# Graph attention layer with sparse experts: edge scores by a masked product and one maximum out of PSUM, with wider target products

## The chip, the cores and the metric

The kernel runs on one core of one Trainium2 chip. The metric is the device time of one execution in microseconds (us). TensorE (PE in the profile; PEld is its weight load), VectorE (DVE), ScalarE (ACT), GpSimd (POOL) and the queue of SyncE (SP) run side by side and wait for each other on semaphores; 16 DMA engines move the data.

## The reference

A graph attention layer over 3125 nodes, 50000 edges and the self loops, and behind it a layer of 8 experts with the top 2 chosen. The change touches the attention scores:

```python
xp = (x @ W).reshape(N, H, C)                      # N = 3125, H = 4, C = 256
a_src = jnp.einsum('nhc,hc->nh', xp, att_src)
a_dst = jnp.einsum('nhc,hc->nh', xp, att_dst)
e = jax.nn.leaky_relu(a_src[src] + a_dst[dst], NEG_SLOPE)
m = jax.ops.segment_max(e, dst, num_segments=N)
ee = jnp.exp(e - m[dst])
z = jax.ops.segment_sum(ee, dst, num_segments=N)
alpha = ee / z[dst]
out = jax.ops.segment_sum(xp[src] * alpha[:, :, None], dst, num_segments=N)
```

Each edge needs four numbers of its source node, `a_src[src]`, and eight (`a_src` and `a_dst`) of its target.

## The kernel before

The program is seven blocks, one after the other, each with its own instruction list for every engine and a barrier behind it. The nodes are cut into 25 blocks of 125 rows (`ROWS`), the edges, sorted by target, into 416 visits of up to 128 edges (`VISITS`), each of which belongs to one block of targets.

**Projection** (block at L303). For each of the 25 node blocks i, TensorE multiplies the normalised rows by W in two 16-bit parts (`body(i)`, L1886), and VectorE takes the sums with `att_src` and `att_dst` out of PSUM (`node_sums`, L508), the low part (`lo_proj`, L493), and normalises the rows of a later block (`moments`, `normed`, `normed_low` L487). TensorE can turn the rows of block i+1 (L1904) only after `normed_low(i+1)`. Between these, VectorE does work for the edges: `edge_numbers` at i = 13 splits each source number into a node block `hi` and a row in it `lo`; `high_one_hots` (L598) at i = 17 to 24 writes `hi_oh`, for each edge a row of 25 zeros and ones; `build_first` (L609, L610) at i = 22 turns the first chunk of numbers into one-hot matrices. SP's queue holds the loads of x in order, the store of `lo` and of the target's row (L327, L328), and last the load of chunk 0 (L332).

**Scores** (block at L760). The visits are cut into 8 chunks of 52, each chunk into 13 groups of 4 (104 groups). A chunk's numbers are loaded by SP (L767): two copies that each write the same 13312 bytes (52 visits of 128 numbers, 16 bits) into all 128 partitions, one of `lo` and one of the target's row. There are two buffers, `stage` and `one_hots`, so the load of chunk i waits until TensorE has done chunk i-2 (`s_grp`). VectorE compares each copy with the partition number, in place (`build`, L776 and L777), and does so for chunk i+1 between groups 8 and 9 of chunk i. `build` waits for the load; the groups behind it on VectorE wait with it.

For each group TensorE forms, per visit, `s_ps` = one-hot of `lo` times all node terms `st16` (125 rows, 25 blocks x 4 heads = 100 columns, a high and a low part: L865, 8 products) and `d_ps` = one-hot of the target's row times the 16 columns of its block (L870, 4 products). VectorE multiplies `s_ps` by `hi_oh` into `pick` (L790) and adds up over the 25 blocks into `sT` (L800). ScalarE copies `d_ps` out (L827). There are two PSUM buffers of each: TensorE starts group n when L790 of group n-2 is done (`s_sel`). During chunks 0 and 1 TensorE also does parts of other products (`gram_part`).

**Behind it** come the maximum over each target's edges (L895), the weighted sums over the edges with indirect gathers (L1039), the node layer (L1180), the routing (L1477) and the experts (L1698). The change does not touch them.

## Time and profile before

| | |
|---|---|
| time, 3 executions | 2158.95, 2160.12 (median), 2163.76 us |
| profiled execution, first to last instruction (its span) | 2296.1 us |
| mean granted clock of TensorE in it | 0.919 |
| scores block in it, from the first load to the last L800 | 332 to 482.6 us |

The profile gives no time of its own for the profiled execution beyond its span; that span is 136 us above the median of the executions without the profiler, so sums are made in microseconds of the span and carried over as differences. The granted clock is in units of 2.4 GHz (0.5 is 1.2 GHz). In a line of the time line the first number is the start, the second the length; `x8` means 8 instructions merged into one line, and what stands in brackets is how long the engine was idle before it and what released it. A line of the table of stretches has, for each engine, the busy time and the count of instructions, then the granted clock, the mean busy share of the 16 DMA engines, and GB/s.

### The profile page before, as it was taken

What the parts mean: (1) busy time and instruction counts of PE and PEld (TensorE: products, weight loads), DVE (VectorE), ACT (ScalarE), POOL (GpSimd) and SP (SyncE); (2) the same over time, 40 slices, a digit from 0 to 9 for tenths busy, and PEclk for the clock granted to TensorE, in tenths of its full rate; (3) what the DMA queues carried; (4) which work ended last, traced back from release to release, by engine and by line L of the source; (5) the groups of instructions that cost most, each with busy time, mean ns of one, the idle gap of its engine ahead of it and who ended that gap; (6) DMA issues with size and microseconds to landing.
All of it is one profiled execution on the core that took longest, in us unless ns stands there. A gap on an engine that the chain in (4) does not pass through costs nothing. (4 is left out here: it accounts for less than half of the span.)

```text
span 2296.1 us, 53233 instructions
## 1 busy us (share of the span) xinstructions
PE 1959.2 (85%) x14846; PEld 1318.7 (57%) x14847; DVE 1470.6 (64%) x4341; ACT 1137.3 (50%) x2499; POOL 768.2 (33%) x943
## 2 busy tenths in 40 slices
PE   6999977667878888888888589983899999999997
PEld 4666545645766667777667455652454445555553
DVE  7988859987666666666666699867543443443333
ACT  4444421113666666676666566654543443443332
POOL 1020000022555555555555232321233333333332
PEclk9999976568999999999999889995899999999999
DMA  7444544403988888888888677746646556644542
GB/s 272 134 143 136 172 131 172 186 0 114 312 281 291 286 299 287 294 296 287 287 298 294 235 249 240 228 142 234 233 169 249 212 167 239 221 160 171 176 162 80
DMA packets 135664, 490.15 MB, mean 213 GB/s; under 512 B 16900, under 2 KB 17108, under 8 KB 133410
## 3 DMA queue, kind: packets, MB, share of 16 engines
q0 software_dynamic: 95568, 334.62, 43.5%
q1 hardware_dynamic: 31954, 125.15, 15.1%
q10 hardware_dynamic: 8064, 29.36, 3.7%
q8 instruction: 47, 0.77, 0.1%
q14 instruction: 31, 0.25, 0.0%
HBM read 419.17 MB, written 81.17 MB: 218 GB/s over the span
## 5 line engine op out<-in xcount | busy, mean ns | idle before, releaser
L1130 PE MATMUL main_ps<-rows,O 128*128 128x256 f16 x4992 | 619.2, 283 | 125.7 <-DVE acc L1066 66.3
L1113 ACT ACTIVATE O<-O,pk 128x128 f16<-128x128 f16 x1664 | 502.9, 387 | 246.1 <-DVE O L1083 203.5
L1130 PEld LDWEIGHTS main_ps<-rows,O 128*128 128x128 f16 x4992 | 480.9, 102 | 217.9 <-issue 72.8
L1052 POOL DMA_INDIRECT rows<-projected,idx x416 | 395.5, 951 | 325.2 <-PE small_ps L1135 202.9
L1087 DVE TENSOR_SCALAR O<-O,pk 128x128 f16<-128x128 f16 x1664 | 314.6, 273 | 15.0 <-issue 0.2
L1837 PE MATMUL x_h<-w_p,gram 128*128 x1344 | 307.1, 386 | 18.4 <-ACT gram L1787 7.6
L1852 PE MATMUL x_o<-w_p,gram 128*128 x1344 | 308.0, 379 | 1.4 <-ACT gram L1806 1.4
L1886 PE MATMUL pj_ps<-gram,xsT 128*125 128x512 f16 x1200 | 271.1, 385 | 8.8 <-ACT xsT L402 5.5
L1837 PEld LDWEIGHTS x_h<-w_p,gram 128*128 128x128 f16 x1344 | 131.6, 99 | 171.6 <-issue 31.5
L1886 PEld LDWEIGHTS pj_ps<-gram,xsT 128*125 128x125 f16 x1200 | 163.2, 139 | 104.7 <-ACT xsT L402 8.6
L1083 DVE TENSOR_SCALAR O<-iota,pk 128x128 f16<-128x128 f16 x416 | 109.4, 263 | 164.9 <-PE small_ps L1135 124.1
L1852 PEld LDWEIGHTS x_o<-w_p,gram 128*128 128x128 f16 x1344 | 129.2, 98 | 147.1 <-issue 1.6
L1795 ACT ACTIVATE h_g<-h_b 128x512 f32<-128x512 f32 x56 | 35.3, 630 | 301.7 <-DVE h_b L1767 301.7
L1732 POOL DMA_INDIRECT out_dram<-x_y,xi x56 | 57.5, 1027 | 349.8 <-DVE x_y L1760 349.8
L1895 PE MATMUL n_pj<-gram,PK 128*128 128x512 f16 (+3 forms) x900 | 156.2, 330 | 13.3 <-ACT PK L1343 13.3
L1757 DVE SCALAR_TENSOR_TENSOR x_o<-x_o,b_t 128x1024 f32<-128x1024 f32 x56 | 69.0, 1233 | 135.4 <-PE x_o L1852 132.2
L1787 ACT ACTIVATE gram<-x_tr 128x2048 f16<-128x2048 f16 x56 | 105.1, 1878 | 58.3 <-PE x_tr L1904 55.0
L1895 PEld LDWEIGHTS n_pj<-gram,PK 128*128 128x128 f16 x900 | 83.8, 99 | 82.5 <-ACT PK L1343 15.9
L1760 DVE SCALAR_TENSOR_TENSOR x_y<-x_o,gate_of_slot,x_y 128x1024 f32<-128x1024 f32 x56 | 71.9, 1284 | 69.4 <-DMA x_y<-out_dram,xi 62.1
L1217 POOL TENSOR_TENSOR PK<-n_xn,PK 125x1024 f16<-125x1024 f32 x25 | 53.3, 2130 | 165.6 <-DVE n_x L1267 151.7
L1767 DVE SCALAR_TENSOR_TENSOR h_b<-x_h,b_b 128x512 f32<-128x512 f32 x56 | 38.7, 690 | 107.1 <-PE x_h L1837 104.3
L378 POOL DMA_DIRECT2D projected_f<-xp_f x25 | 13.2, 527 | 247.7 <-ACT xp_f L396 247.7
(346 smaller groups left out, 2538.9 us busy)
## 6 DMA issues: line engine op xcount, KB each, us to landing
w_f<-in_L_ffn_W_dram SPq DMA_DIRECT2D x14, 2048.0 KB
b_t<-in_L_ffn_b_dram ACTq DMA_DIRECT2D x56, 512.0 KB
projected_f<-xp_f POOLq DMA_DIRECT2D x25, 500.0 KB, 3.7
projected<-xp POOLq DMA_DIRECT2D x25, 500.0 KB, 4.6
out_dram<-n_x SPq DMA_DIRECT2D x25, 500.0 KB
x_after_gnn_normed<-PK POOLq DMA_DIRECT2D x25, 500.0 KB, 9.1
xt<-in_x_dram SPq DMA_DIRECT2D x24, 512.0 KB, 3.3
n_own<-projected_f SPq DMA_DIRECT2D x24, 512.0 KB, 13.0
```

Source lines behind the costliest of these rows:

```text
L1052: pool.indirect_dma_start(out=rows[:, 4 * p + k, :, :].rearrange("k n d -> k (n d)"), out_offset=None, in_=xp_d[:, :], in_offset=bass.Indi ...
L1083: dve.tensor_scalar(O[:, k, 0, :], iota16[:, :], pk[:, p, k, 0:1], None, ALU.is_equal).then_inc(s_oh, 1)
L1087: ins = dve.tensor_scalar(O[:, k, 1 + h, :], O[:, k, 0, :], pk[:, p, k, 1 + h:2 + h], None, ALU.mult)
L1113: ins = act.activation(O[:, k, 1 + HEADS + h, :], O[:, k, 0, :], ACT.Copy, scale=pk[:, p, k, w:w + 1])
L1130: pe.matmul(main_ps[:, h * C:(h + 1) * C], O[:, k, 1 + HEADS * a + h, :], rows[:, 4 * p + k, b, h * C:(h + 1) * C], start=first and h % 2 ...
L1757: dve.scalar_tensor_tensor(o_ps[:, p, :], o_ps[:, p, :], 1.0 / WS, b2_t[:, p, :], ALU.mult, ALU.add).then_inc(s_ob, 1)
L1760: dve.scalar_tensor_tensor(y[:, p, :], o_ps[:, p, :], at1(gateT, i), y[:, p, :], ALU.mult, ALU.add).then_inc(s_eo, 1)
L1787: act.activation(xgT[:, p, :, :, :], tr_ps[:, :, :, :], ACT.Copy).then_inc(s_xT, 1)
L1837: ins = pe.matmul(h_ps[:, :], xgT[:, p, a, k, :], w, start=(k == 0 and a == b), stop=(k == KD - 1 and a == 1))
L1852: ins = pe.matmul(o_ps[:, p, n * 512:(n + 1) * 512], hT[:, p, a, f, :], w, start=(f == 0 and a == b), stop=(f == KF - 1 and a == 1))
L1886: ins = pe.matmul(out, lhs[:, a, k, :], rhs[:, b, k, :], start=(k == 0 and a == b), stop=(k == last - 1 and a == 1))
L1895: ins = pe.matmul(out[:, cols], lhs[:, a, k, :], rhs[:, b, k, cols], start=(k == 0 and a == b), stop=True, skip_group_check=True)
```

## The change

1. The source number is split by 116 in place of 125: `lo` = number within 116 (`LOW`), and the quotient (27 values, `HI`) into two digits, a high one of 3 values and a low one of 9 (`TENS`). The one-hot matrix of 128 rows now holds 116 rows for `lo`, 3 for the high digit and 9 for the low digit (`parts_of`). So the copy of `lo` writes 116 partitions, and two further copies write 3 and 9; the copy of the target's row stays at 128.
2. A matrix `terms` (128 rows, 27 x 4 = 108 columns, two parts) replaces `st16` in the product. Its first 116 rows are the node terms, spread anew by 50 small products at the end of the projection; its last 12 rows hold a large negative number wherever the column's digit is not the row's (`digit_mask`). The product thus gives the wanted terms in one of 27 places and very negative numbers in the others, and one maximum over the 27 out of PSUM (`TENSOR_REDUCE`) replaces the multiplication and the sum. `hi_oh`, `pick` and `high_one_hots` go; TensorE waits for that maximum (`s_got`) in place of L790.
3. The target products read 96 columns (`WIDE`) in place of 16, six node blocks of which the first is the wanted one; ScalarE still copies 16 of each.

```diff
-HI = -(-NODES // P)
+LOW, TENS = 116, 9
+HI = -(-NODES // LOW)
+DIGITS = HI // TENS + TENS
+MASK = -65504.0
...
+        src_row = sbuf(early_ctx, "src_row", [P, 1])
+        terms = sbuf(early_ctx, "src_terms", [P, 2, HI, HEADS], F16)
         dstV = sbuf(early_ctx, "dstV", [VP, ROW4])
-        st16 = sbuf(early_ctx, "node_terms_parts", [ROWS, BLOCKS, 4 * HEADS], F16)
+        AHEAD = WIDE // (4 * HEADS)
+        st16 = sbuf(early_ctx, "node_terms_parts", [ROWS, BLOCKS + AHEAD - 1, 4 * HEADS], F16)
...
+        def parts_of(lo, dl):
+
+            end = LOW + HI // TENS
+            return (lo[0:LOW], lo_d), (lo[LOW:end], third_d), (lo[end:P], unit_d), (dl, dloc_d)
...
+            spread_ps = t_ps[:, :, :].rearrange("p a b -> p (a b)")[:, 0:2 * HI * HEADS].rearrange("p (n a h) -> p n a h", n=2, h=HEADS)
...
+                            sp.dma_start(third_d.rearrange("(p r) n -> p (r n)", r=4), rowV[:, 2, :]).then_inc(s_vstore, 16)
+                            sp.dma_start(unit_d.rearrange("(p r) n -> p (r n)", r=4), rowV[:, 3, :]).then_inc(s_vstore, 16)
+                    sp.wait_ge(s_vstore, 64)
+                    sp.wait_ge(s_tr_ix, 2)
+                    for t, d in parts_of(stage_lo, stage_dl):
+                        sp.dma_start(t, d[0:CHUNK, :].partition_broadcast(t.shape[0])).then_inc(s_row[0], 16)
...
-                        link(dve.tensor_scalar(fV[:, 1, :], fV[:, 0, :], 1.0 / ROWS, -float(ROWS // 2) / ROWS, ALU.mult, ALU.add))
+                        link(dve.tensor_scalar(fV[:, 1, :], fV[:, 0, :], 1.0 / LOW, -0.5 * (LOW - 1) / LOW, ALU.mult, ALU.add))
...
-                        dve.scalar_tensor_tensor(fV[:, 2, :], fV[:, 1, :], -float(ROWS), fV[:, 0, :], ALU.mult, ALU.add)
+                        dve.scalar_tensor_tensor(rowV[:, 0, :], fV[:, 1, :], -float(LOW), fV[:, 0, :], ALU.mult, ALU.add)
+                        link(dve.tensor_scalar(fV[:, 2, :], fV[:, 1, :], 1.0 / TENS, -0.5 * (TENS - 1) / TENS, ALU.mult, ALU.add))
+                        link(dve.tensor_scalar(fV[:, 2, :], fV[:, 2, :], WHOLE, None, ALU.add))
+                        link(dve.tensor_scalar(fV[:, 2, :], fV[:, 2, :], -WHOLE, None, ALU.add))
+                        dve.tensor_copy(rowV[:, 2, :], fV[:, 2, :])
+                        dve.scalar_tensor_tensor(rowV[:, 3, :], fV[:, 2, :], -float(TENS), fV[:, 1, :], ALU.mult, ALU.add)
...
-                    def high_one_hots(n):
-
-                        if n == 0:
-                            dve.wait_ge(s_trc, 2)
-                        vs = slice(n * CHUNK, (n + 1) * CHUNK)
-                        dve.tensor_tensor(hi_oh[:, vs, :], iota16[:, 0:HI].unsqueeze(1).broadcast_to([P, CHUNK, HI]),
-                                          hiT[:, vs].unsqueeze(2).broadcast_to([P, CHUNK, HI]), ALU.is_equal).then_inc(s_hioh, 1)
+                    def digit_mask():
+
+
+                        top = HI // TENS
+                        dve.memset(shift16[:, 0:P], 0.0)
+                        dve.memset(shift16[:, 2 * P:], 0.0)
+                        dve.tensor_copy(shift16[:, P:2 * P], ident)
+                        link(dve.tensor_scalar(digit[:, 0:1], iota_col[:, :], LOW - 0.5, -float(LOW), ALU.is_gt, ALU.mult))
+                        link(dve.tensor_scalar(digit[:, 1:2], iota_col[:, :], LOW + top - 0.5, -float(top), ALU.is_gt, ALU.mult))
+                        link(dve.tensor_tensor(digit[:, 2:3], digit[:, 0:1], digit[:, 1:2], ALU.add))
+                        link(dve.tensor_tensor(src_row[:, :], iota_col[:, :], digit[:, 2:3], ALU.add))
...
+                        link(dve.tensor_scalar(digits_of[:, 0, :], digits_of[:, 2, :], src_row[:, :], digit[:, 3:4], ALU.not_equal, ALU.mult))
+                        for part in range(2):
+                            dve.tensor_copy(mask[:, part, :, :], digits_of[:, 0, :].unsqueeze(2).broadcast_to([P, HI, HEADS]))
...
-                        if i in (15, 17, 19):
+                        if i in (15, 17):
                             turned_numbers((i - 15) // 2)
+                        if i == 16:
+                            digit_mask()
                         if 14 <= i < 14 + KD:
                             low_wp(i - 14)
-                        if 17 <= i < 25:
-                            high_one_hots(i - 17)
...
+                    dve.wait_ge(s_spread, 1)
+                    dve.tensor_copy(terms[:, :, :, :], spread_ps)
...
+                    pe.wait_ge(s_trc, 2)
+                    pe.matmul(spread_ps, ident16[:, :], mask[:, :, :, :], start=True, stop=True, skip_group_check=True)
+                    for n, blocks in enumerate((range(LATE), range(LATE, BLOCKS))):
+                        pe.wait_ge(s_st16, 2 * n + 2)
+                        for b in blocks:
+                            for a in range(ROWS * b // LOW, (ROWS * (b + 1) - 1) // LOW + 1):
+                                w = P - (ROWS * b - LOW * a)
+                                ins = pe.matmul(spread_ps[0:LOW, :, a, :], shift16[0:ROWS, w:w + LOW],
+                                                st16[:, b, :].rearrange("r (n g h) -> r n g h", n=2, g=2)[:, :, 0, :],
+                                                start=False, stop=True, skip_group_check=True)
+                    ins.then_inc(s_spread, 1)
...
-            pick = sbuf(c, "pick", [P, 2, 4, HEADS, HI])
...
-                        for t, d in ((lo_b, lo_d), (dl_b, dloc_d)):
-                            sp.dma_start(t[p], d[CHUNK * i:CHUNK * (i + 1), :].partition_broadcast(P)).then_inc(s_row[p], 16)
+                        for t, d in parts_of(lo_b[p], dl_b[p]):
+                            sp.dma_start(t, d[CHUNK * i:CHUNK * (i + 1), :].partition_broadcast(t.shape[0])).then_inc(s_row[p], 16)
...
-                        dve.wait_ge(s_row[p], 32 * (j + 1))
-                        dve.tensor_scalar(lo_b[p], lo_b[p], iota_col[:, 0:1], None, ALU.is_equal)
+                        dve.wait_ge(s_row[p], 64 * (j + 1))
+                        dve.tensor_scalar(lo_b[p], lo_b[p], src_row[:, 0:1], None, ALU.is_equal)
...
-                            if not early(n, 2):
-                                dve.wait_ge(s_got, n - 1)
                             dve.wait_ge(s_grp, n + 1)
-                            dve.tensor_tensor(pick[:, b, :, :, :], s_ps[b][:, :, :].rearrange("k v (a h) -> k v h a", h=HEADS),
-                                              hi_oh[:, four(n), :].unsqueeze(2).broadcast_to([P, 4, HEADS, HI]), ALU.mult).then_inc(s_sel, 1)
-                            if not early(n, 1):
-                                total(n - 1, 1 - b)
-
-                    def four(n):
-                        return slice(4 * n, 4 * n + 4) if isinstance(n, int) else bass.ds(4 * n, 4)
-
-                    def total(n, b):
-                        dve.wait_ge(s_sel, n + 1)
-                        dve.tensor_reduce(sT[:, four(n), :], pick[:, b, :, :, :], AX.X, ALU.add).then_inc(s_got, 1)
-
-                    dve.wait_ge(s_hioh, 8)
+                            four = slice(4 * n, 4 * n + 4) if isinstance(n, int) else bass.ds(4 * n, 4)
+                            dve.tensor_reduce(sT[:, four, :], s_ps[b][:, :, :].rearrange("k v (a h) -> k v h a", h=HEADS), AX.X, ALU.max).then_inc(s_got, 1)
...
-                        act.activation(d, d_ps[p][:, 0:16 * HEADS].rearrange("k (v n h) -> k v n h", v=4, n=2), ACT.Copy).then_inc(s_got_d, 1)
+                        act.activation(d, d_ps[p][:, 0:4 * WIDE].rearrange("k (v n) -> k v n", v=4)[:, :, 0:4 * HEADS].rearrange("k v (n h) -> k v n h", n=2), ACT.Copy).then_inc(s_got_d, 1)
...
-                                pe.wait_ge(s_sel, n - 1)
+                                pe.wait_ge(s_got, n - 1)
                             for u in range(4):
                                 for part in range(2):
-                                    h0 = 2 * HEADS * part
-                                    pe.matmul(s_ps[(p + q) % 2][:, u, :].rearrange("k (a h) -> k a h", h=HEADS), lo_b[p][0:ROWS, 4 * q + u, :],
-                                              st16[:, :, h0:h0 + HEADS], start=(part == 0), stop=(part == 1))
+                                    pe.matmul(s_ps[(p + q) % 2][:, u, :], lo_b[p][:, 4 * q + u, :],
+                                              terms[:, part, :, :].rearrange("r a h -> r (a h)"), start=(part == 0), stop=(part == 1))
                             if not early(n, 2):
                                 pe.wait_ge(s_got_d, n - 1)
                             for u in range(4):
-                                ins = pe.matmul(d_ps[(p + q) % 2][:, 4 * HEADS * u:4 * HEADS * (u + 1)], dl_b[p][0:ROWS, 4 * q + u, :],
-                                                st16[:, bass.ds(block_of[u], 1), :].squeeze(1), start=True, stop=True)
+                                ins = pe.matmul(d_ps[(p + q) % 2][:, WIDE * u:WIDE * (u + 1)], dl_b[p][0:ROWS, 4 * q + u, :],
+                                                st16[:, bass.ds(block_of[u], AHEAD), :].rearrange("r b n -> r (b n)"), start=True, stop=True)
```

What moves on SP's queue, at the end of the projection and the head of the scores block. Before:

```order
L332 DMA stage<-src_lo_by_visit 128x6656 [waits ix_tr,ix_vstore]
L332 DMA stage<-dst_local_by_visit 128x6656
L767 DMA one_hots<-src_lo_by_visit 128x6656
L767 DMA one_hots<-dst_local_by_visit 128x6656
L767 DMA stage<-src_lo_by_visit 128x6656 [waits ed_grp]
L767 DMA stage<-dst_local_by_visit 128x6656
```

And with the change, in the same place (`src_high_digit_by_visit` and `src_low_digit_by_visit` are the new arrays of digits):

```order
L349 DMA stage<-src_lo_by_visit 116x6656 [waits ix_tr,ix_vstore]
L349 DMA stage<-src_high_digit_by_visit 3x6656
L349 DMA stage<-src_low_digit_by_visit 9x6656
L349 DMA stage<-dst_local_by_visit 128x6656
L818 DMA one_hots<-src_lo_by_visit 116x6656
L818 DMA one_hots<-src_high_digit_by_visit 3x6656
L818 DMA one_hots<-src_low_digit_by_visit 9x6656
L818 DMA one_hots<-dst_local_by_visit 128x6656
L818 DMA stage<-src_lo_by_visit 116x6656 [waits ed_grp]
L818 DMA stage<-src_high_digit_by_visit 3x6656
```

Each load is four copies in place of two, the first of 116 partitions; the wait for `ed_grp` (`s_grp`) stands at the same copy.

What moves on VectorE, around the first `build` of the scores block. Before:

```order
L800 TENSOR_REDUCE sT<-pick 128x16 [waits ed_sel]
L776 TENSOR_SCALAR one_hots<-one_hots,iota_col 128x6656 [waits ed_row1]
L777 TENSOR_SCALAR one_hots<-one_hots,iota_col 128x6656
L790 TENSOR_TENSOR pick<-s_ps,PK 128x400 [waits ed_grp,ed_got]
L800 TENSOR_REDUCE sT<-pick 128x16 [waits ed_sel]
L790 TENSOR_TENSOR pick<-s_ps,PK 128x400 [waits ed_grp,ed_got]
```

With the change:

```order
L840 TENSOR_REDUCE sT<-s_ps 128x16 [waits ed_grp] x8
L827 TENSOR_SCALAR one_hots<-one_hots,src_row 128x6656 [waits ed_row1]
L828 TENSOR_SCALAR one_hots<-one_hots,iota_col 128x6656
L840 TENSOR_REDUCE sT<-s_ps 128x16 [waits ed_grp] x13
L827 TENSOR_SCALAR stage<-stage,src_row 128x6656 [waits ed_row0]
```

One reduction out of `s_ps` stands for each pair of L790 and L800; `build` keeps its place between groups 8 and 9 (the first group is a row of its own, ahead of these) and its wait for the load (`ed_row1`, `ed_row0`).

On TensorE a group of chunk 0 was, before:

```order
L857 TENSOR_LOAD visit_blocks
L865 MATMUL s_ps<-node_terms_parts,stage 128x100 [waits ed_sel]
L865 MATMUL s_ps<-node_terms_parts,stage 128x100 x7
L870 ISA [waits ed_got_d]
L870 MATMUL d_ps<-node_terms_parts,stage 128x16
```

and is now:

```order
L895 TENSOR_LOAD visit_blocks
L902 MATMUL s_ps<-src_terms,stage 128x108 [waits ed_got]
L902 MATMUL s_ps<-src_terms,stage 128x108 x7
L907 ISA [waits ed_got_d]
L907 MATMUL d_ps<-node_terms_parts,stage 128x96
```

The same rows in the same order, with 108 and 96 columns, and `ed_got` in the place of `ed_sel`.

## Rows read from the trace of the kernel before

**Rows 1.** The page: busy us (share of the span) of each engine.

```profile
PE 1959.2 (85%) x14846; PEld 1318.7 (57%) x14847; DVE 1470.6 (64%) x4341; ACT 1137.3 (50%) x2499; POOL 768.2 (33%) x943
```

**Rows 2.** Table of stretches: the scores block.

```profile
332.00:480.00 148.00, 106.83 (x1482) 91.69 (x1483) 136.53 (x229) 24.01 (x106) 0.00 (x0) 0.58 0.41 162
```

**Rows 3.** Instruction groups, 357-480 us: busy us, mean ns | idle.

```profile
L790 DVE TENSOR_TENSOR pick<-s_ps,PK 128x400 f32<-128x400 f32 x90 | 51.6, 574 | 4.2 <-PE d_ps L870 1.1
...
L800 DVE TENSOR_REDUCE sT<-pick 128x16 f32<-128x400 f32 x91 | 50.7, 558 | 0.0
```

**Rows 4.** Time line, 402 to 412 us: groups, a build, the next load's issue.

```profile
402.24 0.63 PEld L865 LDWEIGHTS s_ps<-node_terms_parts,one_hots 125*128 125x128 f16 x8 [0.23 <-DVE pick L790]
...
403.32 0.63 PEld L865 LDWEIGHTS s_ps<-node_terms_parts,one_hots 125*128 125x128 f16 x8 [0.23 <-DVE pick L790]
...
405.06 1.95 DVE L776 TENSOR_SCALAR stage<-stage,iota_col 128x6656 f16<-128x6656 f16 x1 [0.23 <-DMA stage<-dst_local_by_visit]
...
411.47 0.32 SPq L767 DMA_DIRECT2D one_hots<-src_lo_by_visit  x1
```

**Rows 5.** Time line, the next build.

```profile
422.99 1.94 DVE L776 TENSOR_SCALAR one_hots<-one_hots,iota_col 128x6656 f16<-128x6656 f16 x1
```

**Rows 6.** Table of stretches: while a chunk's two copies run.

```profile
413.00:421.00 8.00, 7.19 (x96) 6.49 (x93) 7.50 (x16) 1.79 (x8) 0.00 (x0) 0.50 0.96 399
...
419.00:421.00 2.00, 1.79 (x26) 1.61 (x25) 1.93 (x5) 0.45 (x2) 0.00 (x0) 0.50 1.00 426
```

**Rows 7.** Stretches in which one SP copy runs: 104, 125 and 125 partitions.

```profile
177.00:177.80 0.80, 0.80 (x5) 0.51 (x4) 0.80 (x7) 0.40 (x1) 0.00 (x0) 1.00 0.80 230
...
1304.90:1305.70 0.80, 0.00 (x0) 0.00 (x0) 0.70 (x4) 0.00 (x0) 0.00 (x0) 0.50 0.29 113
...
1525.50:1527.50 2.00, 2.00 (x45) 2.00 (x42) 1.90 (x8) 0.20 (x1) 1.31 (x2) 1.00 0.30 94
```

**Rows 8.** Time line of SP: issues of the two copies of 125 partitions.

```profile
1303.72 0.29 SPq L1183 DMA_DIRECT2D n_bias<-in_L_gnn_bias_dram  x1
...
1524.02 0.27 SPq L1202 DMA_DIRECT2D out_dram<-n_x  x1
```

**Rows 9.** Time line, scores block's head: load 1, build, load 2.

```profile
332.07 0.32 SPq L767 DMA_DIRECT2D one_hots<-src_lo_by_visit  x1
...
350.25 1.94 DVE L776 TENSOR_SCALAR one_hots<-one_hots,iota_col 128x6656 f16<-128x6656 f16 x1
...
356.76 0.32 SPq L767 DMA_DIRECT2D stage<-src_lo_by_visit  x1
```

**Rows 10.** Time line, projection: load of chunk 0, build, TensorE.

```profile
268.81 0.34 SPq L332 DMA_DIRECT2D stage<-src_lo_by_visit  x1
...
277.48 10.75 PE L1886 MATMUL pj_ps<-gram,xsT 128*125 128x512 f16 x48
...
283.44 1.95 DVE L609 TENSOR_SCALAR stage<-stage,iota_col 128x6656 f16<-128x6656 f16 x1 [1.82 <-DMA stage<-dst_local_by_visit]
...
292.34 1.86 PE L1904 MATMUL tr_ps<-ident,xs 125*128 125x125 f16 x16 [4.11 <-DVE xs L487]
...
293.99 12.38 PE L1886 MATMUL pj_ps<-gram,xsT 128*125 128x512 f16 x48
```

**Rows 11.** Waits of TensorE, 130 to 330 us: total, times, longest.

```profile
PE tr_ps L1904 <- DVE xs L487: 6.9, 6, 4.1
```

**Rows 12.** Time line: a VectorE step on 104x512; 24 products of 96 columns.

```profile
172.41 0.43 DVE L548 TENSOR_SCALAR stage<-stage 104x512 f32<-104x512 f32 x1
...
1541.55 1.18 PE L1886 MATMUL n_sc<-Msim,PK 128*128 128x96 f16 x24
```

**Rows 13.** Time line: last build and last sums of the scores block.

```profile
458.54 1.94 DVE L776 TENSOR_SCALAR one_hots<-one_hots,iota_col 128x6656 f16<-128x6656 f16 x1
...
481.60 1.04 DVE L800 TENSOR_REDUCE sT<-pick 128x16 f32<-128x400 f32 x2
```

**Rows 14.** DMA issues: KB each, median us from issue to landing.

```profile
projected_f<-xp_f POOLq DMA_DIRECT2D x25, 500.0 KB, 3.7
```

42 lines of the change are left out of this document (25 added, 17 removed).

## The prediction

> **What bounds the kernel now.** I read the page first, then the table of stretches for the scores block, its instruction groups, and last the time line around one `build`. Over the whole span TensorE is the busiest engine [rows 1], but the change sits in the scores block, and there it is VectorE: 136.5 of 148 us busy, TensorE 106.8, at a mean granted clock of 0.58 [rows 2]. Per group VectorE spends 0.57 us in L790 and 0.56 in L800 [rows 3], which overlap a little; the groups come every 1.08 us, and TensorE sits idle 0.23 us before each, released by L790 [rows 4]. That is the row that invites the change.
>
> The second thing to see is who else is at the edge. The `build` at 405.06 begins 0.23 us late, released by its DMA, not by a VectorE step [rows 4]. The load after it is issued at 411.47 [rows 4] and its `build` begins at 422.99 [rows 5]: 11.5 us. So a chunk's period of 17.9 us (405.06 to 422.99) is as much a loop of loads as of groups: load 11.5, `build` 3.8 (two steps of 1.95, slightly overlapped), 2.6 until TensorE has done groups 11 and 12 and frees the buffer. 11.5 + 3.8 + 2.6 = 17.9. Nothing that shortens groups 0 to 8 shortens this loop. What the copies do inside the 11.5 us: the DMA engines are busy 0.96 to 1.00 of the time, at 399 to 426 GB/s for all 16 [rows 6].
>
> **What the change does to the loads, the main term.** The copy of `lo` is cut from 128 partitions to 116, with copies of 3 and 9 beside it. The bytes are the same; the number of DMA engines is not. A copy of 104 partitions on SP's queue held 0.80 of the engines, which is 13 of 16 (0.81), and 104 = 13 x 8; two of 125 partitions, a broadcast load and a store [rows 8], held 0.29 and 0.30, which is 5 of 16 (0.31), and 125 = 5 x 25; 128 partitions hold all 16 [rows 6, 7]. From these three I take it that a copy on this queue goes to the largest number of engines up to 16 that divides its partitions. 116 = 4 x 29: four engines, 29 rows of 13312 bytes each. Behind them on the same queue stand the copy of 3, that of 9, and 8 rows per engine of the target's copy. The busiest engine carries 29 + 1 + 1 + 8 = 39 rows; before it carried 16.
>
> A row takes 13312 bytes / 26.6 GB/s (426 / 16) = 0.50 us. The nearest other row is the broadcast of 125, 113 GB/s on 0.29 x 16 = 4.6 engines, 24.4 GB/s each, 0.55 us a row [rows 7]. I take 0.50, because it is the same copy with the same row length. Then 23 more rows are 11.5 us, and a load takes 23.0 (39 x 0.50 and the same 3.5 of issue and landing). The trace does not show whether the small copies share their engines with the 29 rows; if not, 37 rows, 22.0 us. That and 0.55 are the ends: 10.5 to 12.7 us more per load.
>
> The Trainium skill, "DMA: Bandwidth & Descriptors", section "Why a DMA increments its semaphore by 16 and not by 1", says that on the hardware queues a copy takes the lowest-numbered engines. By that rule the small copies do share, the sum stays at 39 rows, and the end with 37 falls away; no row here shows it.
>
> **The terms, in us, against the profiled span.**
> - Load 1 (scores block). Issued at 332.07, needed at 350.25 [rows 9]. It now lands at 332.07 + 23.0 = 355.1: +4.8.
> - Loads 2 to 7: each is waited for from its issue to its `build`, as shown. 6 x 11.5 = +69.0 (63 to 76). VectorE, TensorE and ScalarE all stand in that wait, since TensorE can be only two groups ahead of VectorE.
> - VectorE's saving, 104 x about 0.5 us, falls into that wait: 13 groups at about 1.1 us are 14 of the new 29.4 us of a period. What hides it is the load; without it, it would be the first rival below.
> - TensorE's added columns: a group had 8 x 100 + 4 x 16 columns, now 8 x 108 + 4 x 96 = 1248. At 1.2 GHz, which the 0.50 of these stretches is [rows 6], that is 1.04 us; at 2.4 GHz 24 products of 96 columns took 1.18 us [rows 12], so 12 take 0.55 to 0.6. In chunks 1 to 6 it hides under the load too. The two groups between `build` and the next issue become 0.56 + 0.1 + 2 x 1.05 = 2.8 at the low clock, before 2.6; at the high one 1.8. I take no change (-5 to +1 in all).
> - Behind the last `build`. From 458.54 to the last L800 at 482.6 it was 24.1 us [rows 13], 17 groups of them. At 1.2 GHz TensorE needs 1.05 a group, nothing is gained; if the clock comes up, up to 17 x 0.48 = 8. After an idle load wait TensorE starts low, so I take a quarter: -2 (-8 to 0).
> - Load of chunk 0 (projection). Issued at 268.81, `build_first` began at 283.44 after 1.82 us of waiting for it, and TensorE then stood 4.11 us for `xs`; its next 48 products took 12.38 us where they had taken 10.75 [rows 10]. The wait is exposed already, so the 11.5 comes on top: VectorE has `node_sums`, `lo_proj` and `normed_low` queued behind it, and TensorE waits for the last. TensorE's idle 4.1 becomes about 16, and I add 2 for a longer stretch at half clock. +13.5 (11 to 17).
> - `high_one_hots` gone. TensorE waited 6.9 us for `xs`, of which 4.1 is the wait above [rows 11]; the other 2.8 were caused by these steps. -3 (-4 to 0).
> - More number work: five steps on 104x512, as the 0.43 us one [rows 12], at i = 13, 2 us, and 18 tiny ones at i = 16, each between nothing and that 0.43, say half, 4 us. What hides both is that VectorE is a step ahead of TensorE there; if that cover is gone, +6. I take +1.
> - The two further stores of digits follow the same wait on SP's queue; the loads of x behind them have an iteration in hand: 0. The 50 spreading products at the end of the projection run while VectorE does the last sums and POOL the last stores: 0 (up to +2).
>
> Sum: 4.8 + 69.0 + 0 - 2 + 13.5 - 3 + 1 = **+83 us**. The profiled span would go from 2296 to 2379. The timed executions are 136 us shorter than that span; a wait for a transfer should be as long in them, so I carry the difference over: 2160 + 83 = **2243 us** (+3.8%). A difference of 0.2% is about what a measurement of this kernel can tell from none.
>
> **Rivals.**
> 1. Faster: SP's copies are dealt out over all 16 engines whatever their partitions. POOL's store of 125 rows, 500 KB, lands in a median of 3.7 us [rows 14], over 135 GB/s, more than five engines at 24.4 carry, so that queue does deal this way. The Trainium skill, in the same section, tells of such an exception for the software queue only; the trace agrees in both rows. Then the busiest engine has 8 + 1 + 1 + 8 = 18 rows, load 12.5, and with the high clock a period of 12.5 + 3.8 + 1.8 = 18.1: six times +0.2, the end -8, the projection (+1 for its load, -3, +1) -1: -8, **2152 us**. It decides if SP's copy of 116 shows a DMA share near 1.0. Against it: the 0.29 and 0.30, on this very queue. Chance 0.07.
> 2. Dealt evenly, but the clock stays at 1.2 GHz: TensorE becomes the bound with 1.05 us a group, period 12.5 + 3.8 + 2.8 = 19.1, six times +1.2, nine groups of chunk 0 at +0.3, projection -1: +9, **2169 us**. For it: the clock was 0.50 while TensorE was busy nine tenths. Chance 0.04.
> 3. Worse than forecast: four engines move only as much each as in the store of 125 rows, 94 / 4.8 = 19.6 GB/s [rows 7], 0.68 us a row. Load 3.5 + 39 x 0.68 = 30.0: 11.8 for load 1, 6 x 18.5 = 111, 20.5 in the projection, less 4: +139, **2299 us**. Against it: that was a write to memory, the loads are reads. Chance 0.05.
>
> **How the numbers follow.** The forecast, slower by 83, has 0.84. Its own range: all low ends together give 3.8 + 63 - 5 - 8 + 10.5 - 4 = +60, all high ones 6 + 76 + 1 + 17 + 6 + 2 = +108. 2218 to 2272 holds nearly all of it, and leaves the three rivals out. Faster by over 0.2% is rival 1 but for its errors, 0.06; same, what is left of rivals 1 and 2 near zero, 0.02; slower 0.92.
>
> **What would show it.** While the copy of 116 runs, the DMA share is 0.25 and the rate near 105 GB/s, after a first stretch with all engines; the landing of the target's copy goes from 11 to about 22 us; `build` waits some 12 us on `dst_local`'s or `lo`'s DMA, seven times; its period is 29 us; `TENSOR_REDUCE` takes about 0.6 us and never waits long except for `build`; TensorE's wait for `xs` at the end of the projection is near 16 us. The forecast is wrong if the share of that copy is near 1, or if the period stays at 18 us.

## The result, and the profile after

| | before | after |
|---|---|---|
| time, median (us) | 2159.67 (2158.95 to 2163.76, 4 runs) | 2273.97 (2269.27 to 2286.09, 4 runs) |
| ratio, 95% interval | | 1.053 (1.0497 to 1.0563) |
| profiled span (us) | 2296.1; of a second profile 2151.0 | 2267.6 |
| block of edge scores (us) | 150.5 | 252.0 |

Slower by 114 us, where 83 were forecast; 2274 lies 2 us above the range's end of 2272. The profiled span of before, 2296, was 136 us longer than its timed runs. A second profile of the same kernel, 2151.0, shows where most of it lies: in the weighted sums, which the change does not touch and on which no term rests, 752 us for 624. The waits of SP, which span the blocks (us in total, times, longest), first profile of before:

```profile
SPq L1039 <- PEq L1039: 752.3, 1, 752.3
```

The second profile of before, and the kernel after (the same place in its code):

```profile
SPq L1039 <- PEq L1039: 623.6, 1, 623.6
```

```profile
SPq L1076 <- PEq L1076: 622.9, 1, 622.9
```

So blocks are compared here, not spans. The table of stretches of after: the scores block, then the parts of one load (us, busy time of PE, PEld, DVE, ACT, POOL, clock, DMA share, GB/s).

```profile
343.00:595.00 252.00, 106.44 (x1488) 87.39 (x1488) 92.40 (x130) 24.13 (x107) 0.00 (x0) 0.68 0.35 95
380.00:388.00 8.00, 7.72 (x107) 5.64 (x105) 4.31 (x8) 1.67 (x8) 0.00 (x0) 1.00 0.91 205
388.00:390.00 2.00, 1.35 (x21) 1.12 (x21) 1.12 (x2) 0.35 (x2) 0.00 (x0) 1.00 0.53 157
390.00:404.00 14.00, 1.18 (x15) 0.90 (x15) 0.00 (x0) 0.45 (x2) 0.00 (x0) 0.63 0.26 97
```

Against [rows 2] VectorE fell from 136.5 us busy in 148 to 92.4 in 252, and TensorE's busy time stayed at 106, with more columns at a higher granted clock (0.68 for 0.58): the edit did to the two engines what it was written to do. The time went to the load. Fourteen of its microseconds have a DMA share of 0.26, four engines of 16, and in them TensorE is busy 1.2 us and VectorE not at all; before, a load had a share of 0.96 over the 8 us of [rows 6]. The second thing to read here is the first line of the load. All engines are at work, 0.91, but move 205 GB/s and not 399 to 426: rows nearly twice as long. That is what the forecast did not have.

The builds of after in the time line, to be held against [rows 4] and [rows 5]:

```profile
405.20 1.95 DVE L827 TENSOR_SCALAR stage<-stage,src_row 128x6656 f16<-128x6656 f16 x1 [15.77 <-DMA stage<-dst_local_by_visit]
...
438.98 1.95 DVE L827 TENSOR_SCALAR one_hots<-one_hots,src_row 128x6656 f16<-128x6656 f16 x1 [17.20 <-DMA one_hots<-dst_local_by_visit]
```

and the first issues of three loads on SP:

```profile
343.38 0.25 SPq L818 DMA_DIRECT2D one_hots<-src_lo_by_visit  x1
...
378.30 0.25 SPq L818 DMA_DIRECT2D stage<-src_lo_by_visit  x1
...
411.88 0.24 SPq L818 DMA_DIRECT2D one_hots<-src_lo_by_visit  x1
```

From 378.30 to 405.20 is 26.9 us, from 411.88 to 438.98 is 27.1. A chunk takes 33.8 us (build to build) where it took 17.9. VectorE's waits for these loads:

```profile
DVE one_hots L827 <- DMA one_hots<-dst_local_by_visit: 54.7, 4, 17.2
DVE stage L827 <- DMA stage<-dst_local_by_visit: 50.7, 3, 17.7
```

Seven waits, 105.4 us. The eighth load is the one in the projection: VectorE waits 19.65 us for it, and TensorE, for the `xs` behind, 19.70 (before 1.82 and 4.11 [rows 10]).

```profile
295.53 1.95 DVE L648 TENSOR_SCALAR stage<-stage,src_row 128x6656 f16<-128x6656 f16 x1 [19.65 <-DMA stage<-dst_local_by_visit]
```

```profile
304.42 1.86 PE L1941 MATMUL tr_ps<-ident,xs 125*128 125x125 f16 x16 [19.70 <-DVE xs L505]
```

The operation that replaced the product and the sum of [rows 3]:

```profile
L840 DVE TENSOR_REDUCE sT<-s_ps 128x16 f32<-128x432 f32 x104 | 62.2, 606 | 53.5 <-PE d_ps L907 53.2
```

0.61 us a group in place of 1.13.

### The profile page after: what moved, and what is told of

The parts are those of the page before. It is cut to its first block and busy times, and to the rows that moved or that the text cites. A ratio compares the mean times of both kernels' runs of the same rounds, so it can differ in the third digit from the quotient of the medians.

```text
span 2267.6 us, 53157 instructions
## 1 busy us (share of the span) xinstructions
PE 1901.3 (84%) x14894; PEld 1293.5 (57%) x14895; DVE 1420.2 (63%) x4253; ACT 1134.6 (50%) x2499; POOL 774.2 (34%) x943
## 3 DMA queue, kind: packets, MB, share of 16 engines
q1 hardware_dynamic: 32188, 125.36, 16.5%
## 5 line engine op out<-in xcount | busy, mean ns | idle before, releaser
L1167 PE MATMUL main_ps<-rows,O 128*128 128x256 f16 x4992 | 573.2, 273 | 46.4 <-DVE acc L1103 28.7
L1167 PEld LDWEIGHTS main_ps<-rows,O 128*128 128x128 f16 x4992 | 464.1, 98 | 112.6 <-DVE acc L1103 33.8
L1120 DVE TENSOR_SCALAR O<-iota,pk 128x128 f16<-128x128 f16 x416 | 116.6, 280 | 55.7 <-PE small_ps L1172 26.4
L865 ACT ACTIVATE d_p<-d_ps 128x64 f32 (+1 forms) x104 | 23.4, 225 | 236.7 <-PE d_ps L907 236.7
L902 PE MATMUL s_ps<-src_terms,stage 128*128 128x108 f16 x416 | 36.3, 245 | 82.1 <-DVE sT L840 66.4
```

The source lines that it names most:

```text
L1120: dve.tensor_scalar(O[:, k, 0, :], iota16[:, :], pk[:, p, k, 0:1], None, ALU.is_equal).then_inc(s_oh, 1)
L1167: pe.matmul(main_ps[:, h * C:(h + 1) * C], O[:, k, 1 + HEADS * a + h, :], rows[:, 4 * p + k, b, h * C:(h + 1) * C], start=first and h % 2 ...
```

## The experiments

Eighteen runs. In the table "rate" is what the stretch shows in a load's first part, while the lo copy or both run; "load" is from SP's first issue to the build that needs it, the mean of the loads of chunks 2 to 7; "period" from build to build, the mean of five (of four in e6). All are read from the time lines and tables of stretches. The time is the median of 4 to 10 executions in before, after, e1, e4, e5, e8 and e9; the others ran once.

| run | copies, partitions | rate, GB/s (share) | load, us | period, us | time, us |
|---|---|---|---|---|---|
| before | 128, 128 | 399 to 426 (0.96 to 1.0) | 11.6 | 17.9 | 2159.7 |
| after | 116, 3, 9, 128 | 205 (0.91) | 27.1 | 33.8 | 2274.0 |
| e1 | 112, 2, 14, 128 | 240 (1.02) | 14.6 | 21.3 | 2178.2 |
| e2 | 116, 12, 128, code of before | 223 (0.99) | 28.3 | 34.7 | 2283.1 |
| e3 | 128 first, 116, 3, 9 | 389 (1.02), then 92 (0.24) | 25.2 | 32.1 | 2257.6 |
| e4 | 128, 128, then 3, 9 over it | 422 (1.02) | 13.0 | 19.7 | 2164.7 |
| e5 | as e4, build later | as e4 | hidden | 16.3 | 2142.8 |
| e6 | as after, build later | | 33.5 | 27.1 | 2222.3 |
| e7 | 112, 16, 128, code of before | 240 (0.99) | 13.9 | 20.2 | 2171.1 |
| e8 | as e5, 16 columns | as e5 | hidden | 16.5 | 2141.9 |
| e9 | as before, build later | | hidden | 17.7 | 2158.8 |
| e10 | 116, 3, 9 alone | 100 (0.26) | 19.5 | 26.3 | 2229.5 |
| e11 | 128 and 128 on two queues | 407 (0.97) | 11.7 | 18.0 | 2166.8 |
| e12 | as after, one source | 216 (0.95) | 26.9 | 33.6 | 2277.0 |
| e13 | 116, 128 | 229 (1.04) | 25.9 | 32.7 | 2263.9 |
| e14 | 112, 112, 16, 16 | 283 (0.98) | 16.9 | 23.3 | 2196.5 |
| e15 | 104, 104 | 173 (0.81) | 17.7 | 24.0 | 2198.7 |
| e16 | 112, 112 | 300 (1.03) | 13.0 | 19.4 | 2169.3 |
| e17 | 104, 128 | 213 (1.00), then 359 (0.85) | 14.3 | 20.6 | 2171.2 |

**e0_before**, the kernel before, once more with a profile.

> The kernel before, profiled anew. Its first trace spans 2296 us, 136 above its times, and its block of weighted sums shows 752 us against 623 in the trace of the changed kernel, though neither kernel differs there. If that was a disturbance of one execution, this trace spans about 2160 to 2165 us, the block takes about 620, and the scores block again 150. If the block really is slower before, it stays near 750.

2152.8 us. Its weighted sums take 623.6 us, as shown above. Its scores block begins at 329.74 us, that of the first profile at 332.07: where the block begins is known to some 2 us.

**e1_low112**: is it the number of partitions?

```diff
-LOW, TENS = 116, 9
+LOW, TENS = 112, 14
```

> The changed kernel with 112 rows of lo, 2 of the high digit and 14 of the low one in place of 116, 3 and 9: the same computation, one line. Theory (rows on the busiest DMA engine): 7 + 1 + 1 + 8 = 17 rows in place of 39, a load of 12 us in place of 26.9, a period of 18 to 19 us in place of 34, in all 2150 to 2170 us. Rival (the number of copies, or the wider products, make the kernel slower): near 2274 us.

2178.24 us, ratio to before 1.0089 (1.0061 to 1.0116). One number gives back 96 of the 114 us; everything else of the change is still in. It missed its expectation by 8 us all the same: a load takes 14.6 us, not 12, with all 16 engines busy:

```profile
424.00:432.00 8.00, 5.87 (x97) 4.78 (x95) 4.85 (x8) 1.79 (x8) 0.00 (x0) 0.99 1.02 240
```

**e2_old_split**: is it anything else of the change? The kernel before with its lo copy cut in two, in chunk 0 as well.

```diff
-for t, d in ((lo_b, lo_d), (dl_b, dloc_d)):
-    sp.dma_start(t[p], d[...].partition_broadcast(P))
+for t, d in ((lo_b[p][0:116], lo_d), (lo_b[p][116:P], lo_d), (dl_b[p], dloc_d)):
+    sp.dma_start(t, d[...].partition_broadcast(t.shape[0]))
```

> The kernel before with only its copy of lo cut in two, 116 and 12 partitions, of the same array; everything else as before. Theory: 29 + 1 + 8 = 38 rows on the busiest engine, a load of 26 us, 2260 to 2275 us. Rival (the new arithmetic or the small arrays matter): 2160 us.

2283.1 us. The kernel of before, its arithmetic untouched, becomes slower than after by the cut alone. Its build, against [rows 5]:

```profile
514.24 1.95 DVE L776 TENSOR_SCALAR one_hots<-one_hots,iota_col 128x6656 f16<-128x6656 f16 x1 [16.47 <-DMA one_hots<-dst_local_by_visit]
```

With e1 this settles where the 114 us come from. The size of a load, 27.1 for 23.0, was still open.

**e3_target_first**: do the target's rows slow down when they run beside the 116?

```diff
-return (lo[0:LOW], lo_d), (lo[LOW:end], third_d), (lo[end:P], unit_d), (dl, dloc_d)
+return (dl, dloc_d), (lo[0:LOW], lo_d), (lo[LOW:end], third_d), (lo[end:P], unit_d)
```

> The changed kernel with the target's copy (128 partitions) issued ahead of the three others. The busiest engine still has 39 rows. In the changed kernel all 16 engines were busy for the first 8 us of a load at only 213 GB/s, a row taking 0.86 us and not 0.50. Theory A (the two copies disturb each other while they run side by side): issued in this order they hardly overlap, rows take 0.50, a load 23 us, in all 2274 - 8 x 3.9 = 2243 us. Theory B (rows are slower whenever few engines carry most of the work): no change, 2270 to 2278 us.

2257.6 us, between the two. The target's rows now run at the old rate, and then comes the copy on four engines, with a slow seam between them:

```profile
474.00:478.00 4.00, 3.71 (x54) 3.40 (x51) 2.55 (x5) 0.89 (x4) 0.00 (x0) 0.73 1.02 389
478.00:480.00 2.00, 1.39 (x26) 1.13 (x24) 1.22 (x2) 0.45 (x2) 0.00 (x0) 1.00 0.18 47
480.00:496.00 16.00, 2.53 (x44) 1.99 (x40) 1.22 (x2) 0.89 (x4) 0.00 (x0) 0.70 0.24 92
```

So side by side the two copies do cost each other time. A load gets only 1.8 us shorter where theory A had 3.9; the seam at 47 GB/s and rows at 92 GB/s (97 in the kernel after) take back the rest.

**e4_overwrite**: the change with an even copy. All 128 partitions are loaded from `lo_d`; the digits go over rows 116 to 127 when that has landed.

```diff
-return (lo[0:LOW], lo_d), (lo[LOW:end], third_d), (lo[end:P], unit_d), (dl, dloc_d)
+return (lo, lo_d), (dl, dloc_d), (lo[LOW:end], third_d), (lo[end:P], unit_d)
...
-for t, d in parts_of(lo_b[p], dl_b[p]):
+for n, (t, d) in enumerate(parts_of(lo_b[p], dl_b[p])):
+    if n == 2:
+        sp.wait_ge(s_low[p], 16 * (i // 2 + 2))
```

> The changed kernel with rows 0 to 127 of the lo copy loaded as one copy of all 128 partitions (as before the change), and the two small copies (3 and 9 partitions) written over its rows 116 to 127 once it has landed; nothing else moved. Theory (the four engines that carry 116 partitions are the whole loss): a load takes 12.5 to 14 us from issue to build, the period of a chunk falls from 34.0 to 19.5 to 20.5 us, 2155 to 2172 us in all. Rival (four copies of a load, or small ones, cost by their number): a load stays over 18 us and the time over 2200.

2164.74 us, ratio 1.0015 (1.0005 to 1.0026): the rate is back, a load takes 13.0 us, and four copies a load cost little by their number.

```profile
436.00:442.00 6.00, 4.15 (x71) 3.44 (x71) 3.65 (x6) 1.34 (x6) 0.00 (x0) 1.00 1.02 422
```

What is left is the change without its loss, and it is no gain: the loop of load 13.0, build 3.8 and 2.9 until the buffer is free sets its period, whatever VectorE saves.

**e5_over_later**: the loop taken apart.

```diff
-if q == GR - 4 and not (isinstance(i, int) and i == 7):
+if q == GR - 2 and not (isinstance(i, int) and i == 7):
```

> The same with VectorE's build of the next chunk put two groups before the chunk's end instead of four, so that TensorE finishes the chunk, and SP issues the load after the next, without waiting for that build. Theory: the load is no longer in one chain with the build, VectorE's own work (one maximum of 0.61 us a group, 13 groups, and the build) or TensorE's 13 groups set the period, 14 to 17 us against 17.95 before the change; 2125 to 2145 us in all, under the kernel before. Rival (the chain load, build, products stays, since only two buffers are there): the period stays 19 to 20 us and the time within 5 us of the run without the later build.

2142.78 us, ratio **0.9915** (0.9898 to 0.9931), the first version that beats both. TensorE finishes a chunk, and SP issues the load after the next, without waiting for the build between them. No build waits for a load:

```profile
417.32 1.95 DVE L832 TENSOR_SCALAR one_hots<-one_hots,src_row 128x6656 f16<-128x6656 f16 x1
...
433.48 1.95 DVE L832 TENSOR_SCALAR stage<-stage,src_row 128x6656 f16<-128x6656 f16 x1
```

16.2 us here: 13 groups at 1.04 and 2.6 more in which TensorE waits for the end of the build.

**e6_later_build**: the same edit, alone, on the kernel after.

> The changed kernel, its copies unchanged, with the build two groups before the chunk's end instead of four. Theory: a load still takes 26.9 us, but loads follow each other without the 7 us of build and products between them: period 28 to 29 us, 2235 to 2245 us. Rival (the load slows when its predecessor is still under way, since the same four engines carry both): 33 to 34 us a chunk and 2270 us as before.

2222.3 us, 13 us better than the better expectation: period 27.1 instead of 33.8. The load's own time is now hidden in part behind the one before. Its stretches hold a hint on the open question. In its load from 371 on, all 16 engines move 206 to 235 GB/s, as in the kernel after; at 396 to 398, when two loads overlap, the rate is whole:

```profile
396.00:398.00 2.00, 0.00 (x0) 0.00 (x0) 0.00 (x0) 0.00 (x0) 0.00 (x0) 0.50 1.00 419
```

The build at 399.96 waits for the load before, whose last rows on the four engines are the target's. If the order of a queue's rows on an engine is the order of issue, then at that moment all 16 engines carry rows of copies of 128 partitions.

**e9_old_later**: is the place of the build a gain by itself? Same edit, kernel before.

> The kernel before the change with its build put two groups before the chunk's end instead of four. Theory (its VectorE, with a product and a sum for each group, sets the period of 17.95 us, and no build waits over 0.23 us for a load): nothing to gain, 2155 to 2163 us. Rival (the place of the build alone made the gain of the fastest version): 2135 to 2150.

2158.84 us, ratio 0.9995 (0.9982 to 1.0008): nothing. The two edits of e5 need each other: the later build takes the load out of the loop, and only the single maximum lets the period fall below 17.7.

**e8_over_later_narrow**: e5 with the target products back to 16 columns.

```diff
-st16[:, bass.ds(block_of[u], AHEAD), :].rearrange("r b n -> r (b n)")
+st16[:, bass.ds(block_of[u], 1), :].squeeze(1)
```

ScalarE's copy reads the narrower PSUM rows accordingly.

> The fastest version so far (lo copy of 128 partitions with the small ones written over it, later build) with the target products back to 16 columns; everything else is the same. Theory of the widening (the added columns keep TensorE's clock up, and cost little): the granted clock of the scores block falls below its 0.88, groups follow each other at over 1.04 us, and the time rises by 3 to 15 us, to 2146 to 2158. Rival (the columns are work and nothing else): a group gets 0.05 to 0.15 us shorter at the same clock, and the time falls to 2128 to 2138.

2141.93 us, ratio to before 0.9924 (0.9898 to 0.9949), against 0.9915 of e5: no difference. The scores stretch of e5, then of e8:

```profile
343.00:468.00 125.00, 89.96 (x1300) 75.65 (x1298) 85.87 (x118) 22.95 (x102) 0.00 (x0) 0.88 0.46 172
```

```profile
343.00:468.00 125.00, 92.45 (x1264) 80.48 (x1263) 85.63 (x117) 22.87 (x101) 0.54 (x1) 0.70 0.45 172
```

The widening does raise the granted clock, 0.88 for 0.70. The theory was right on that and wrong on what it is worth: with a sixth of the columns in the target products and the lower clock TensorE is busy 92.5 us instead of 90.0, and the period is 16.5 us for 16.3. The time lines say why the clock buys nothing. Two groups of e5, then of e8:

```profile
429.06 0.56 PE L907 MATMUL s_ps<-src_terms,one_hots 128*128 128x108 f16 x8 [0.32 <-issue]
...
430.09 0.56 PE L907 MATMUL s_ps<-src_terms,one_hots 128*128 128x108 f16 x8 [0.29 <-issue]
```

```profile
425.84 0.90 PE L907 MATMUL s_ps<-src_terms,one_hots 128*128 128x108 f16 x8
...
426.86 0.90 PE L907 MATMUL s_ps<-src_terms,one_hots 128*128 128x108 f16 x8
```

The groups start 1.03 and 1.02 us apart here, 1.04 in the mean of a chunk in either run. In e5 the products are done sooner, and TensorE then stands 0.3 us marked "issue", for nothing that the profile shows. What holds the groups at 1.04 us no run separates.

**e7_old_112_16**: is every cut slow? The kernel before, lo copy as 112 and 16.

> The kernel before the change with its lo copy of 128 partitions issued as two, of 112 and of 16 partitions; the same rows into the same places. Both spread over all 16 engines, so the even share stays. Theory (a row costs more when the engines are out of step with each other, as between copies of 7 and 8 rows an engine): a load takes 14 us instead of 12.5, of which the kernel before hides most: 2160 to 2175 us. Rival (rows cost 0.5 us whatever their neighbours do): 2155 to 2160 us, load 12.5 to 13 us.

2171.1 us, load 13.9, as its theory expected (the theory itself falls below, with e14). All 16 engines are busy, and the rows are slow until the target's are alone:

```profile
399.00:407.00 8.00, 7.11 (x92) 6.50 (x92) 7.72 (x16) 1.56 (x7) 0.00 (x0) 0.50 0.99 240
407.00:411.00 4.00, 3.12 (x43) 2.75 (x40) 2.88 (x6) 0.89 (x4) 0.00 (x0) 0.50 0.88 367
```

**e10_lo_only** and **e11_two_queues**: the uneven copy without a neighbour, and two even copies side by side, the target's issued by ScalarE.

```diff
-for t, d in parts_of(lo_b[p], dl_b[p]):
+for t, d in parts_of(lo_b[p], dl_b[p])[0:4 if i == 1 else 3]:
```

> The changed kernel without the target copies of chunks 2 to 7 (their target one-hots are left out of the computation, the old ones stay); the lo copy of 116 partitions and the two small ones as they are. Theory (rows on the four engines take 0.50 us when no other copy runs beside them): 29 rows and the 3.5 us around them make a load of 18 us, a period of 25 us, some 2220 us in all. Rival (rows of this uneven copy are slow by themselves at its start): a load of 21 us or more, and 2240 us.

> The kernel before the change with the target copy issued by ScalarE on its own queue at the same moment as SP issues the lo copy, so that the two run side by side on all 16 engines with even shares. Theory A (two copies that read different places of HBM at once slow each other's rows, whatever their shares): rows take 0.8 to 1.0 us, a load 16 to 19 us, the time 2180 to 2210 us. Theory B (it takes engines with different shares or out of step, two sources alone cost nothing): a load stays 12 to 13.5 us and the time 2155 to 2165.

e10: 2229.5 us, load 19.5, 100 GB/s on four engines, 0.53 us a row, and no slow start (81 to 115 GB/s in any 2 us of it). The expectation of 18 had forgotten its own small copies: (29 + 1 + 1) x 0.50 + 3.5 is 19.0. e11: 2166.8 us, 2 above the range of theory B, with a load of 11.7 us, as before, and rows of 0.51 us.

```profile
409.00:423.00 14.00, 6.05 (x96) 4.94 (x96) 4.12 (x7) 2.32 (x10) 0.00 (x0) 0.84 0.26 100
```

```profile
397.00:403.00 6.00, 5.32 (x70) 4.88 (x71) 5.79 (x12) 1.17 (x6) 0.00 (x0) 0.50 0.97 407
```

Neither the copy of 116 alone nor two copies of 128 side by side makes rows slow. Here it takes both.

**e12_same_source** (target copy reads `lo_d` too) and **e13_no_small** (no copies of 3 and 9 from chunk 2 on).

```diff
-(lo[end:P], unit_d), (dl, dloc_d)
+(lo[end:P], unit_d), (dl, lo_d)
```

> The changed kernel with the target copy reading the same table as the lo copy (its one-hots of the targets are then those of the sources' low digit, so the sums by target are left wrong); copies, sizes and destinations are unchanged. Theory (two sources read at once by engines of different shares conflict in HBM): rows of 0.5 us in the first part too, over 350 GB/s there, a load of 23 us, 2243 to 2252 us in all. Rival (the sources do not matter): about 213 GB/s in the first 8 us, a load of 26 to 27 us, 2265 to 2278 us.

> The changed kernel without the small copies of 3 and 9 partitions in the loads of chunks 2 to 7 (their digits stay those of chunks 0 and 1, so the scores of later chunks are left wrong). Theory (the small copies put the engines out of step and keep the rows slow): over 350 GB/s in the first part, a load of 22.5 to 23.5 us, 2243 to 2252 us. Rival (they do nothing beyond their own rows): a load of 26 to 27 us, 2262 to 2276 us.

e12: 2277.0 us and 216 GB/s, so the sources do nothing. e13: 2263.9 us, 229 GB/s, a load of 25.9: the small copies cost 1.2 us of a load, about the 1.0 of their two rows on a busiest engine.

```profile
450.00:458.00 8.00, 5.87 (x98) 4.90 (x96) 4.25 (x7) 1.79 (x8) 0.00 (x0) 1.00 0.95 216
```

```profile
447.00:453.00 6.00, 4.26 (x72) 3.49 (x70) 3.68 (x7) 1.35 (x6) 0.00 (x0) 1.00 1.04 229
```

**e14_in_step**: kernel before, lo 112, target 112, lo 16, target 16.

> The kernel before the change with each of its two copies of 128 partitions cut into 112 and 16, issued as lo 112, target 112, lo 16, target 16: 7, 7, 1 and 1 rows an engine, so that both large copies have the same shares. Theory of step (rows slow down when the copies under way have different shares or start positions): back to rows of 0.50 to 0.54 us, a load of 12.5 to 13.2 us, 2157 to 2166 us. Rival (7 partitions between the engines instead of 8 make the rows slow): rows of 0.65 us or more, a load of 14 to 16 us, 2170 to 2185 us.

2196.5 us, slower than its rival's range too. Copies with the same shares are slow as well, so it does not take engines out of step:

```profile
413.00:423.00 10.00, 8.85 (x114) 8.06 (x115) 9.66 (x19) 2.21 (x10) 0.00 (x0) 0.50 0.98 283
```

**e15_both104**, **e16_both112**, **e17_lo104**: kernel before, its copies of chunks 2 to 7 cut to 104 and 104, 112 and 112, 104 and 128 partitions, nothing in place of the rest.

```diff
-for t, d in ((lo_b, lo_d), (dl_b, dloc_d)):
-    sp.dma_start(t[p], d[...].partition_broadcast(P))
+for t, d, k in ((lo_b, lo_d, P if i == 1 else 104), (dl_b, dloc_d, P if i == 1 else 104)):
+    sp.dma_start(t[p][0:k], d[...].partition_broadcast(k))
```

> The kernel before the change with both copies of chunks 2 to 7 cut to partitions 0 to 103 (the rest keep what chunks 0 and 1 left, so those scores are left wrong): 13 engines if the share is 8 rows each, partitions 8 apart. Theory of spacing (rows are fast where the engines write partitions 8 apart): rows of 0.50 to 0.52 us, about 345 GB/s in the middle of a load, the load 12 to 12.8 us, 2153 to 2162 us in all. Rival (anything but 128 partitions is slow): rows of 0.65 us or more, under 280 GB/s, a load of 14 us or more.

> The same with partitions 0 to 111: 16 engines, 7 rows each, partitions 7 apart, and no small copies at all. Theory of spacing: rows of 0.65 to 0.75 us, 260 to 320 GB/s, the load 12.6 to 14 us for 14 rows an engine. Rival (the extra copies of 16 partitions slowed the rows of the run in step): rows of 0.50 us, about 420 GB/s, the load 10.5 to 11 us, shorter than with 104 partitions.

> The same with 104 partitions in the lo copy and all 128 in the target copy: 16 rows on 13 engines and 8 on three, all of them 8 partitions apart. Theory of spacing: unequal shares cost nothing by themselves, over 390 GB/s while all engines carry rows, the load 12 to 13 us. Rival (unequal shares make the rows slow): 213 to 300 GB/s in that part, the load 15 us or more.

```profile
430.00:443.00 13.00, 8.76 (x115) 7.87 (x113) 8.73 (x17) 2.23 (x10) 0.00 (x0) 0.50 0.81 173
```

```profile
437.00:446.00 9.00, 7.93 (x104) 7.12 (x102) 8.72 (x18) 1.79 (x8) 0.00 (x0) 0.50 1.03 300
```

```profile
441.00:448.00 7.00, 6.20 (x81) 5.66 (x80) 6.76 (x14) 1.47 (x7) 0.00 (x0) 0.50 1.00 213
448.00:451.00 3.00, 2.14 (x30) 1.86 (x28) 1.86 (x4) 0.67 (x3) 0.00 (x0) 0.50 0.85 359
```

e16 fits the spacing theory to the number, and e15 fells it: 13 engines (0.81) with 8 rows of a copy each, and 173 GB/s, 13.3 an engine and 1.0 us a row, half the rate. Fewer bytes than before, and a load of 17.7 us in place of 11.6. (That each engine takes 8 neighbouring partitions is the theory's own assumption; no record shows it.) e17 shows the same copy dragging the three engines along that carry only the target's rows: 213 GB/s over 16 engines is 13.3 each. From 448 on, when 13 engines have 8 rows left, the rate is 26.4 an engine (359 on 0.85 x 16): by the order of issue these are the target's. Its load was 14.3 us, in neither range; its rate is the rival's.

## Why the prediction was wrong

| term | forecast, us | measured, us |
|---|---|---|
| projection (load 0, one-hots, number work) | +11.5 | +11.3 |
| load 1 | +4.8 | +8.8 |
| loads 2 to 7 | +69.0 | +95.5 |
| behind the last build | -2 | -2.9 |
| sum | +83 | +113 |

Measured terms: the scores block starts at 343.38 for 332.07; its first build comes 27.0 us after that for 18.2; from there to the last build is 203.8 us (370.34 to 574.17) for 108.3; to the block's end 21.2 for 24.1. That the first term agrees is in part luck: TensorE's wait for `xs` was 19.7 us where 16 were expected, and the 2 us added for a half clock did not come (the 48 products behind it took 11.63 us, before 12.38), while TensorE had come to that place 3.5 us earlier (its products before the wait end at 284.7 for 288.2). The last term agrees by luck too, as shown below.

**The direction and the mechanism held.** Every step on counts was right: the copy of 116 goes to four engines (0.26 of 16, 97 to 106 GB/s), each of seven builds waits for it, the loop of load, build and two groups sets the period, VectorE's saving falls into the wait, and the added columns of the target products cost nothing (e8; the step from 100 to 108 in `s_ps` was not run by itself). That the small copies share the engines of the 29 rows, 39 rows and not 37, e13 bears out: removing them takes 1.2 us from a load. e10 does not decide it: 19.5 us is 31 rows at 0.52, or 29 at 0.55. The Trainium skill, "DMA: Bandwidth & Descriptors", section "Why a DMA increments its semaphore by 16 and not by 1", has it that on hardware queues a copy goes to the lowest-numbered engines of the core. The sharing that follows from this agrees with the 1.2 us of e13; which engines they are by number no run here shows. Rivals 1 and 2 needed a share near 1 and fall. Rival 3, 0.68 us for all 39 rows and +139, is too large, and has the wrong place: while the four engines work alone, rows take 0.55 (97 GB/s on four engines).

**The step that failed** is "I take 0.50, because it is the same copy with the same row length". The price came from a stretch in which all 16 engines carried copies of 128 partitions, and was put on rows that share the queue with another kind. In the first 8 us of a load, while the 116 and the target's copy run together, a row takes about twice that (205 GB/s on 0.91 x 16 engines is 14 each, 0.95 us). Over a whole load the 39 rows came out at (27.1 - 3.5) / 39 = 0.61 us. As an estimate from these rates, about 8 of the 29 rows on a busiest engine lie in the slow part, 0.45 us more each, 3.6 of the missing 4.1 us. The rows behind them at 0.55 in place of 0.50 would be 1.5 more, so the split is rough, but the greater part is the slow start. Seven loads 4.1 us longer are 29 of the 30.5 us that loads 1 to 7 took beyond the forecast. The range went by the nearest rows, 0.50 and 0.55, and the one row with another price, 0.68 in a store, was put away as a rival at 0.05. One line ahead of the prediction held a warning: the first of [rows 7], used only for its share of 0.80, shows 230 GB/s with 12.8 engines busy, 18 each, not 26.6; a row of 13312 bytes at that rate would take 0.74 us. It is no clean price, though. The stretch is not one copy but two stores of 104 partitions under way together, of 104 KB each, 1 KB a row, and only 0.8 us long:

```profile
176.02 0.34 SPq L327 DMA_DIRECT2D src_lo_by_visit<-stage  x1
176.40 0.37 SPq L328 DMA_DIRECT2D dst_local_by_visit<-stage  x1
```

**The range was also added up too low.** 12.7 us prices only the 23 added rows at 0.55. All 39 at 0.55 are a load of 25.0, 13.4 more; that lifts the upper sum from 108 to about 114, to 2274 us. (The lower sum takes 10.5 for the projection where the term itself says 11.) The measured time would then have touched the range, but by a price that the slow part of a load does not have.

**A second price was wrong, and the sum hid it.** The prediction has a group at 0.55 to 0.6 us where the clock is high, from 24 products in 1.18 us [rows 12]. After the last build of the kernel after, where the mean granted clock is 0.90 and the stretches from 582 on show 1.00, groups still start 1.02 to 1.06 us apart:

```profile
588.84 0.56 PE L902 MATMUL s_ps<-src_terms,one_hots 128*128 128x108 f16 x8 [0.30 <-issue]
...
589.86 0.56 PE L902 MATMUL s_ps<-src_terms,one_hots 128*128 128x108 f16 x8 [0.29 <-issue]
```

The -2.9 us there came from elsewhere: 17 groups took 17.4 us behind the build where VectorE had needed 20.2 for them before. A gain of up to 8 us from the clock, as the forecast allowed, was not to be had.

## What stays open

What makes rows slow is not settled. Shown: copies of 128 partitions run at 26.6 GB/s an engine, in one queue or two; the copy of 116 comes near it alone, 25 on each of four engines (e10). Slow are copies of 112 (283 to 300 GB/s on 16 engines, about 18 each) and of 104 (13.3 each), by themselves, and 128-partition copies while a 116 or 104 is under way (13 to 14 each). Not the cause: different sources (e12), the small copies (e13), two copies at once (e11). Unequal shares are not needed for it (e14 to e16 are slow with equal ones), nor are shares other than 8 rows an engine (e15). TensorE and VectorE's use of the buffers is not it either, as in e15 the rate stays at 168 to 173 when both are idle, after 440. How rows are laid to partitions and engines inside a copy no record shows, and a copy of 64 or 96 partitions was not tried. So one rival stands untested: the engines may hold each other up where they write, depending on which partitions they write at the same moment. It could give 128 fast and 104 slow, but it is a guess; loading the same 104 rows into other partitions would test it. Whether the slow copies of 112 and 104 and the slow rows beside the 116 have one cause or two is open as well.
